# Turning the second experts' rows among the last output tiles, moving the gathered sums, and storing in four parts

## The chip, the cores and the metric

The kernel runs on one core of one Trainium2 chip. The metric is the device time in microseconds. Before the change it is 1516.37 us, the median of three runs (1516.31 to 1519.39).

## What is computed

The input is 1250 nodes with 512 features, and 40,000 edges sorted by their target. Four blocks follow each other, each added to its own input:

```python
x = x + _L0_gnn_ref(_layernorm(x), edge_index_t)      # means over segments, copied back
x = x + _L0_ffn_ref(_layernorm(x)[None], ...)[0]      # 8 experts of width 1536, top 2
x = x + _L1_gnn_ref(_layernorm(x), edge_attr_4, edge_attr_8, edge_index, ...)
x = x + _L1_ffn_ref(_layernorm(x)[None], expert_weights, expert_indices, w1, w2)[0]
```

The change lies in the last two. The third block forms eight blocks of 128 message features per edge, sums them by target node, and multiplies the sums by two output matrices:

```python
msg0 = segment_sum(m0, receiver); msg1 = segment_sum(m1, receiver)
o0, o1 = _lin_irreps(msg0, msg1, W_out0, W_out1)
out = concatenate([o0, o1.reshape(num_nodes, 3 * MUL)], -1) / 10
```

The fourth block has only 512 drawn assignments of two experts each, so only the first 512 nodes get something from it:

```python
for e in range(8):
    h = gelu(xg @ w1[e])                              # 512 -> 256
    y = where(bin_ids == e, h @ w2[e], y)             # 256 -> 512
out = zeros((T, hs)).at[token_ids].add(w * y)
```

## The kernel before

The five engines have one instruction list each (`vector`, `scalar`, `tensor`, `gpsimd`, `sync`), written out by hand, and each runs its list in order. Semaphores set the order between engines; there is no planner. Nodes lie in ten tiles of 128 rows (`NT` = 10), the last with 98. `T5` = 4 is the number of tiles that the second experts work on.

**The edge loop** (lines 1029 to 1041, 1719 to 1736 and others) goes through 88 steps. Each step forms messages for 512 edges from node rows that GpSimd gathers into four buffers of 128 x 1024 values, `gat_pair` (line 328), and sums them with products on TensorE. VectorE adds each step's sum to a running one, and SyncE writes each running sum to the DRAM tensor `sums` (line 2111).

**The output tiles.** When the loop is through, GpSimd gathers for each node tile the rows of `sums` that belong to it, in three buffers `sums_in` in turn (line 1956). TensorE transposes a gathered tile in eight blocks (`turn_sums`, line 1772), ScalarE copies the result out of PSUM in two halves (line 1426), and TensorE forms 16 products with the output weights (`out_products`, line 1780) and a last product in two parts that brings in one extra row (line 1801). VectorE adds the result to `xs`, in two operations of different layout (lines 1089 and 1093). TensorE's list has `turn_sums` of tile t + 1 ahead of the products of tile t, so it doesn't wait for ScalarE's copy of the tile at hand. Banks 0 to 3 of PSUM hold turned sums, banks 4 and 5 the outputs.

After tile 3, the last of the four that the second experts need, VectorE runs the layer norm of these four (`layer_norm(range(T5))`, lines 441 to 480), ScalarE takes the square root for it, and both split the first expert's weights in a high and a low part (lines 1405, 1411, 1065, 1073). Products of 32-bit floats are formed in three passes over such parts (`PASSES`).

**Turning the second experts' rows.** Behind the last output tile, TensorE transposes the four normed tiles `ln[:, t]`, four blocks each (line 1810), into banks 0 and 1 in turn. ScalarE copies each to the high half of `x_hl` (called `nodes_hl` in the profile, line 1435), and VectorE subtracts that from the bank to get the low half (line 1106). From the third tile on TensorE waits for the subtraction of the tile but one before, whose bank it takes.

**The second experts.** TensorE then waits until all four low halves are there and all ten tiles' outputs are added (`v_xt`, `v_o`). For each of eight experts it forms two hidden halves of 12 products each (line 1822), which ScalarE puts through a gelu and copies (lines 1443, 1447) and VectorE subtracts from (line 1125); then 24 products for the four output tiles (line 1833), in banks 4 to 7 in turn, which VectorE multiplies by the coefficient and adds to `xs` (line 1134). The coefficients are made by 17 small operations (lines 1111 to 1118) behind the last subtraction. SyncE stores rows 512 and up when all ten outputs are added (lines 2117, 2119), and the first 512 rows in one transfer when all additions of all experts are done (line 2127); then it waits for all stores.

`phase_tensors` gives out SBUF of a phase: tensors of different calls lie over each other, from the same address. `sums_in` and the two `edge_weights` tensors came from one such call, `x_hl` and its neighbours from another, so gathered sums and turned rows shared memory. `spin` (line 1453) issues products whose result nobody reads.

Of the kernel before, what the change touches and what calls it, by code (L numbers as in the profile page):

```python
# [8 lines left out]
F32 = mybir.dt.float32  # L9
# [3 lines left out]
ALU = mybir.AluOpType  # L13
ACT = mybir.ActivationFunctionType
# [3 lines left out]
NP, NT = 128, 10  # L18
# [25 lines left out]
NTILE = -(-((NE - NW) // TILE + NW) // BT) * BT  # L44
STEPS = NTILE // Q
# [5 lines left out]
MUL, HID = 128, 64  # L51
SILU_2MOM = 1.679177
T1, E1, H1 = 512, 8, 256
T5 = T1 // NP
# [7 lines left out]
NGAT, NSUM, NPICK, NHOT, HOT_STEPS = 8, 3, 3, 2, 4  # L62
# [3 lines left out]
NORMS = (range(0, 3), range(3, 6), range(6, NT))  # L66
LATE_ROWS = 4
MLP_AT = 4
PASSES = ((0, 0), (0, 1), (1, 0))
CHUNKS = [("up", b, k) for b in range(HB) for k in range(4)] + [("down", b, k) for b in range(HB) for k in (0, 2)]  # L70
NCH = len(CHUNKS)
# [7 lines left out]
def search_tree():  # L79

    lo, hi, levels = np.array([0]), np.array([NE]), []
    for _ in range(SEARCH_LEVELS):
# [10 lines left out]
              ident=128, ones=128, before=128, valid=NT, part=1, quarter_tile=STEPS + 2, quarter_hot=Q, node_in=1,  # L93
# [59 lines left out]
def program(nc, consts, x, anc, sub, leaf_table, src, dst, ea4, ea8, gate, w13, w2, w_up, w_mlp1, w_mlp23,  # L153
            w_mlp4, w_out, ew, ei, v1, v2, out):
    ctx = ExitStack()
    with ctx:
# [28 lines left out]
        def phase_tensors(**sizes):  # L185

            with ExitStack() as phase:
                return [phase.enter_context(nc.sbuf_tensor(n, [128, words], dt))[:, :]
                        for n, (words, dt) in sizes.items()]

        pairs = [ctx.enter_context(nc.psum_tensor(f"pair{i}", [128, 1024], F32)) for i in range(4)]
        banks = [pair[:, h * 512:(h + 1) * 512] for pair in pairs for h in range(2)]
# [3 lines left out]
        for name, w in CONSTS.items():  # L196
            K[name] = cst[:, at:at + w]
            at += w
        ident, ones, before = K["ident"], K["ones"], K["before"]
        xs_at = top[0]  # L200
        xs = carve(NT * D).rearrange("p (t d) -> p t d", t=NT)
        ln_at = top[0]
        pair_row = carve(NT * ROW).rearrange("p (t d) -> p t d", t=NT)
        ln, node_id, first_pick = pair_row[:, :, 0:D], pair_row[:, :, D].bitcast(I32), pair_row[:, :, D + 1]
# [32 lines left out]
                for i in range(4)]  # L237
# [31 lines left out]
                                           for _ in range(5))  # L269
# [24 lines left out]
        _, other_up1b, other_down0 = phase_tensors(other_gap0=(4096, F32), other_up1b=(2048, F32),  # L294
                                                   other_down0=(2048, F32))
        _, other_down1 = phase_tensors(other_gap1=(2048, F32), other_down1=(2048, F32))
# [7 lines left out]
        late = zone_of(lnT_at + 4 * NPAD - LATE, LATE)  # L304
        wup_sb, m23_sb, m4_sb, wo_sb = late(2 * MUL), late(2 * HID), late(512), late(512)

        *sums_in, w_copy0, w_copy1 = phase_tensors(**{f"sums_in{i}": (8 * MUL, F32) for i in range(3)},
                                                   edge_weights0=(2 * MUL, F32), edge_weights1=(2 * MUL, F32))
        w_copy = (w_copy0, w_copy1)
        recs = carve(NREC * REC, edge_at).rearrange("p (s c) -> p s c", c=REC)  # L310
        table = dram("node_table", [N, 4 * MUL])
# [6 lines left out]
        ring = zone_of(zone, ZONE - 2048)  # L318
# [6 lines left out]
        msg_pair = [m.rearrange("p (t b u) -> p t b u", t=2, b=8) for m in msg_pair]  # L325
        run_sum = [ring(8 * MUL) for _ in range(NSUM)]
        act1, act2, fT, act3 = ring(512), ring(512), ring(128), [ring(512) for _ in range(2)]
        gat_pair = [ring(1024).rearrange("p (t m u) -> p t m u", t=2, m=4) for _ in range(NGAT // 2)]
        sums = dram("sums", [STEPS * NP, 8 * MUL])
        sum_pair, tp_pair, mlp_pair = pairs[0], pairs[1:3], pairs[3]  # L330
        tp_bank = banks[2:6]
# [6 lines left out]
        x_hl, a1_hl, a2_hl, h_hl0, h_hl1 = phase_tensors(  # L338
            nodes_hl=(2 * 4 * T1, F32R), w_in_hl=(2048, F32R), w_out_hl=(2048, F32R), second_hidden_hl0=(1024, F32R),
            second_hidden_hl1=(1024, F32R))  # L340
        x_hl = x_hl.rearrange("p (s k n) -> p s k n", s=2, k=4)
# [23 lines left out]
        d_store = sem("stored")  # L365
# [69 lines left out]
        def vector(v):  # L435
# [225 lines left out]
            for lv in range(SEARCH_LEVELS - TOP):  # L661
                n = 2 ** lv
# [406 lines left out]
            def split_out(e):  # L1069
                v.wait_ge(a_w2, e + 1)  # L1070
                if e:
                    v.wait_ge(p_y, T5 * e)
                v.tensor_tensor(out=a2_hl[:, 1].rearrange("p k d -> p (k d)"), in0=e_w[e % 2][:, 1024:2048],
                                in1=a2_hl[:, 0].rearrange("p k d -> p (k d)").bitcast(F32),
                                op=ALU.subtract).then_inc(v_w2, 1)
# [6 lines left out]
            v.tensor_copy(out=extra_out, in_=banks[4][:, :]).then_inc(v_extra, 1)  # L1082
            T.wait()
            out_scale = (SILU_2MOM / 8) / 16 / 10
            for t in range(NT):
                r, bank = rows(t), banks[4 + (t + 1) % 2]
                v.wait_ge(p_o, t + 1)
                T.wait()
                T.did(v.scalar_tensor_tensor(out=xs[:r, t, 0:MUL], in0=bank[:r, 0:MUL], scalar=out_scale,
                                             in1=xs[:r, t, 0:MUL], op0=ALU.mult, op1=ALU.add))  # L1090
                xv = xs[:r, t, MUL:].rearrange("p (u m) -> p m u", m=3)
                T.wait()
                T.did(v.scalar_tensor_tensor(out=xv, in0=bank[:r, MUL:].rearrange("p (m u) -> p m u", m=3),  # L1093
                                             scalar=out_scale, in1=xv, op0=ALU.mult, op1=ALU.add), v_o, t + 1)
                if t < T5:
                    block_stats(t)
                if t == T5 - 1:
                    layer_norm(range(T5))
                    split_in(0)
                    split_out(0)  # L1100


            for t in range(T5):
                v.wait_ge(a_xt, t + 1)
                T.wait()
                T.did(v.tensor_tensor(out=x_hl[:, 1, :, t * NP:(t + 1) * NP],  # L1106
                                      in0=banks[t % 2][:, :].rearrange("p (k n) -> p k n", k=4),
                                      in1=x_hl[:, 0, :, t * NP:(t + 1) * NP].bitcast(F32), op=ALU.subtract), v_xt, t + 1)
            v.wait_ge(d_ew, 32)
            T.wait()  # L1110
            T.did(v.tensor_copy(out=ei_sb, in_=ei_sb.bitcast(I32)))
# [27 lines left out]
        def scalar(a):  # L1139
# [279 lines left out]
            for u in range(NT + 1):  # L1419
                a.wait_ge(p_sums_T, u + 1)  # L1420
                if u == 2:
                    a.wait_ge(p_extra, 1)
                if u > 2:
                    a.wait_ge(p_o, u - 2)
                for h in range(2):
                    done = a.activation(out=sums_T[u % 2][:, h * 512:(h + 1) * 512], in_=banks[2 * (u % 2) + h][:, :],  # L1426
                                        func=ACT.Copy)
                done.then_inc(a_sums_T, 1)
                if u == T5 + 1:
                    root(range(T5))  # L1430
                    split_in(0)
                    split_out(0)
            for t in range(T5):
                a.wait_ge(p_xt, t + 1)
                a.activation(out=x_hl[:, 0, :, t * NP:(t + 1) * NP],
                             in_=banks[t % 2][:, :].rearrange("p (k n) -> p k n", k=4),
                             func=ACT.Copy).then_inc(a_xt, 1)
            for e in range(E1):
                for h in range(2):
                    a.wait_ge(p_h, 2 * e + h + 1)  # L1440
# [11 lines left out]
        def tensor(pe):  # L1452
# [312 lines left out]
            def turn_sums(u):  # L1765
                if u:
                    pe.wait_ge(d_sin[(u - 1) % 3], 16 * ((u - 1) // 3 + 1))
                rows_in = sums_in[(u - 1) % 3] if u else run_sum[(STEPS - 1) % NSUM]
                if u >= 2:
                    pe.wait_ge(a_sums_T, u - 1)  # L1770
                for b in range(8):
                    tr = pe.transpose(out=banks[2 * (u % 2) + b // 4][:, b % 4 * 128:(b % 4 + 1) * 128],  # L1772
                                      in_=rows_in[:, b * 128:(b + 1) * 128], identity=ident)
                tr.then_inc(p_sums_T, 1)

            def out_products(bank, u, last=True):
# [5 lines left out]
                                       start=k == n == 0, stop=True, skip_group_check=True)  # L1782
                return mm

            turn_sums(0)
            pe.wait_ge(a_sums_T, 1)
            out_products(banks[4], 0).then_inc(p_extra, 1)
# [2 lines left out]
            for t in range(NT):  # L1790
                bank = banks[4 + (t + 1) % 2]
                if t + 2 <= NT:
                    turn_sums(t + 2)
                pe.wait_ge(a_sums_T, t + 2)
                if t >= 2:
                    pe.wait_ge(v_o, t - 1)
                out_products(bank, t + 1)
                if t == 0:
                    pe.wait_ge(v_extra, 1)
                    pe.wait_ge(v_ehot, 1)  # L1800
                pe.matmul(out=bank[:, :], lhsT=extra_hot[:, t * NP:(t + 1) * NP], rhs=extra_out, start=False,  # L1801
                          stop=True, skip_group_check=True).then_inc(p_o, 1)


            for t in range(T5):
                pe.wait_ge(v_norm, NT // 2 + t + 1)
                if t >= 2:
                    pe.wait_ge(v_xt, t - 1)
                for k in range(4):
                    tr = pe.transpose(out=banks[t % 2][:, k * 128:(k + 1) * 128], in_=ln[:, t, k * 128:(k + 1) * 128],  # L1810
                                      identity=ident)
                tr.then_inc(p_xt, 1)
            pe.wait_ge(v_xt, T5)
            pe.wait_ge(v_o, NT)
            for e in range(E1):
# [22 lines left out]
        def gpsimd(g):  # L1838
# [108 lines left out]


            g.wait_ge(v_sumrow, 1)
            g.wait_ge(d_zero, 32)  # L1950
            for q in range(NSUM):
                g.wait_ge(d_sum[q], 16 * ((STEPS - 1 - q + NSUM - 1) // NSUM))
# [7 lines left out]
        def sync(s):  # L1960
# [161 lines left out]
            for e in range(2, E1):  # L2122
                s.wait_ge(v_w1, e - 1)
                s.wait_ge(v_w2, e - 1)
                load_second(e)
            s.wait_ge(v_y, E1 * T5)
            s.dma_start(out=out[0:T5 * NP].rearrange("(t p) d -> p t d", p=NP), in_=xs[:, 0:T5]).then_inc(d_store, 16)
            s.wait_ge(d_store, 48)
            s.wait_ge(d_fill, 16)
            s.wait_ge(d_zero, 32)  # L2130

# [55 lines left out]
```

## Time and profile before

| | before |
|---|---|
| median of 3 runs | 1516.37 us |
| the profiled execution | 1517.24 us |
| its span | 1515.4 us |
| mean granted clock of TensorE | 0.966 |
| TensorE busy | 1378.3 us (91%) |
| VectorE busy | 1207.7 us (80%) |
| ScalarE busy | 1026.6 us (68%) |
| GpSimd busy | 990.2 us (65%) |
| data moved by DMA | 316.66 MB |

The profile is of one execution, which took 1517.24 us; the span of 1515.4 us lies between its first and its last recorded instruction. The chain of waits goes back from the last instruction, at each step to what released it. PE is TensorE, PEld its weight loads, DVE VectorE, ACT ScalarE, POOL GpSimd, SP SyncE. The granted clock is a share of full speed, 1.00 being 2.4 GHz and 0.50 being 1.2 GHz.

### The profile page before, as it was taken

The page shows a single profiled execution, that of the slowest core. Times are in us where ns is not written, and L with a number is a line of the kernel's source. Part 1 is how long each engine was busy: PE and PEld are TensorE (multiplying, and loading weights), DVE is VectorE, ACT ScalarE, POOL GpSimd, SP SyncE. Part 2 cuts the span into 40 slices and gives each one's busy share as a digit, 9 for nine tenths or more (in the row PEclk, how much of TensorE's full clock was granted, in tenths as well). Part 3 has the DMA queues.
Part 4 walks back from the last instruction along what each step waited for, and adds up shares of the span by engine and source line. Part 5 has one row for each costly group of instructions (what it writes and reads, how often), then busy time and mean ns, then how long its engine had stood idle before and what let it go on. Part 6 is the DMA issues. An engine that isn't in the chain of part 4 may idle for free. (4 is left out here: it accounts for less than half of the span.)

```text
span 1515.4 us, 26210 instructions
## 1 busy us (share of the span) xinstructions
PE 1378.3 (91%) x8774; PEld 837.2 (55%) x8774; DVE 1207.7 (80%) x1633; ACT 1026.6 (68%) x2442; POOL 990.2 (65%) x850
## 2 busy tenths in 40 slices
PE   5858989998899989999896899999999999988998
PEld 3545737885388846887384533333333333336786
DVE  7888818995299936998198499999999999995464
ACT  6347718884288825887183689989989888883343
POOL 4136647888688888888871278878887888772000
PEclk9859999999899999999999999999999999999999
DMA  9338393559445955473523588888888888885321
GB/s 338 133 154 269 106 372 87 162 175 381 125 134 166 346 191 176 138 261 110 184 52 122 174 263 274 285 277 277 277 283 265 277 272 279 277 269 171 115 86 56
DMA packets 90990, 316.66 MB, mean 209 GB/s; under 512 B 23642, under 2 KB 25876, under 8 KB 80747
## 3 DMA queue, kind: packets, MB, share of 16 engines
q1 hardware_dynamic: 45208, 202.57, 36.1%
q0 software_dynamic: 45648, 112.41, 27.8%
q8 instruction: 71, 1.16, 0.3%
q14 instruction: 63, 0.52, 0.1%
HBM read 378.96 MB, written 77.16 MB: 301 GB/s over the span
## 5 line engine op out<-in xcount | busy, mean ns | idle before, releaser
L1883 POOL DMA_INDIRECT sorted_edges<-arena x320 | 473.3, 1479 | 105.5 <-issue 97.7
L898 DVE TENSOR_TENSOR weights_hl<-arena,weights_hl 128x1024 fp32r<-128x1024 f32 x342 | 405.2, 1222 | 62.4 <-ACT weights_hl L1222 59.7
L1930 POOL DMA_INDIRECT arena<-node_table,arena x352 | 337.5, 959 | 135.2 <-issue 40.5
L1222 ACT ACTIVATE weights_hl<-arena 128x1024 fp32r<-128x1024 f32 x342 | 351.9, 1059 | 46.7 <-PE pair L1582 46.5
L1380 ACT ACTIVATE arena<-arena 128x32 f32<-128x32 bf16 x1408 | 359.0, 342 | 2.1 <-DVE arena L1008 2.1
L1582 PE MATMUL pair<-weights_hl,rows_hl 128*128 128x512 f32 x1368 | 326.2, 396 | 4.4 <-DVE rows_hl L903 1.7
L1029 DVE TENSOR_TENSOR arena<-pair,arena 128x768 f32<-128x768 f32 x352 | 317.9, 942 | 0.0
L1582 PEld LDWEIGHTS pair<-weights_hl,rows_hl 128*128 128x128 f32 x1368 | 251.8, 188 | 70.1 <-DVE weights_hl L898 10.6
L1719 PE MATMUL pair<-arena 64*128 64x512 f32 x704 | 189.8, 627 | 24.2 <-DVE arena L1029 23.4
L1582 PE MATMUL pair<-weights_hl,hidden_hl 128*128 128x512 f32 x684 | 165.8, 396 | 0.0
L917 DVE TENSOR_TENSOR arena<-pair,arena 128x512 f32<-128x512 f32 x69 | 47.3, 685 | 125.3 <-ACT arena L1260 97.5
L1582 PEld LDWEIGHTS pair<-weights_hl,hidden_hl 128*128 128x128 f32 x684 | 125.0, 188 | 25.5
L1736 PE MATMUL pair<-arena 128*32 128x256 f32 x2112 | 131.3, 379 | 0.0
L1260 ACT ACTIVATE arena<-pair 128x512 f32<-128x512 f32 x69 | 41.4, 599 | 125.1 <-PE pair L1619 111.3
L1736 PEld LDWEIGHTS pair<-arena 128*32 128x32 f32 x2112 | 75.4, 110 | 77.1 <-issue 51.5
L1719 PEld LDWEIGHTS pair<-arena 64*128 64x128 f32 x704 | 56.8, 187 | 106.1 <-ACT arena L1316 42.2
L1041 DVE SCALAR_TENSOR_TENSOR arena<-arena,pair 128x1024 f32<-128x1024 f32 x88 | 111.3, 1265 | 3.4 <-PE pair L1736 3.4
L1619 PE MATMUL pair<-arena 128*64 128x512 f32 x352 | 96.6, 661 | 18.2 <-DMA arena<-in_w 18.2
L1733 PE MATMUL pair<-arena 128*32 128x512 f32 x704 | 94.6, 608 | 14.4 <-POOL arena L1919 6.9
L1022 DVE TENSOR_TENSOR arena<-pair,arena 128x512 f32<-128x512 f32 (+1 forms) x176 | 95.6, 543 | 12.8 <-DMA arena<-node_table,arena 10.7
L1893 POOL DMA_INDIRECT node_sums<-arena x27 | 55.1, 2040 | 58.9 <-ACT arena L1268 51.9
L1919 POOL TENSOR_TENSOR arena<-edge_weights,arena 128x256 f32<-128x256 f32 x88 | 66.7, 758 | 5.9 <-DMA arena<-node_table,arena 4.4
(289 smaller groups left out, 1531.4 us busy)
## 6 DMA issues: line engine op xcount, KB each, us to landing
arena<-in_w SPq DMA_DIRECT2D x77, 2048.0 KB, 11.5
arena<-in_w SPq DMA_DIRECT2D x77, 1024.0 KB, 8.3
sums<-arena SPq DMA_DIRECT2D x88, 512.0 KB, 6.9
other_down<-in_w SPq DMA_DIRECT2D x8, 1024.0 KB, 10.4
arena<-in_v SPq DMA_DIRECT2D x16, 512.0 KB, 4.6
pair_rows<-arena SPq DMA_DIRECT2D x1, 5934.0 KB, 26.3
arena<-pair_rows SPq DMA_DIRECT2D x23, 256.0 KB, 3.5
arena<-node_table,arena POOLq DMA_INDIRECT x352, 4.8
```

Of the source, the lines that this page charges most:

```text
L898: v.tensor_tensor(out=part[s][:, 1], in0=by_chunk(n)[4], in1=part[s][:, 0].bitcast(F32), op=ALU.subtract).then_inc(v_low, 1)
L1022: v.tensor_tensor(out=m[:, 0:n, 0:2], in0=tp[:, :].rearrange("p (t w u) -> p t w u", t=2, w=4)[:, 0:n, 0:2], in1=rows_in[:, 0:n, 0:1].to_b ...
L1029: v.tensor_tensor(out=m[:, t, 2:8].rearrange("p (w m) u -> p w m u", w=2), in0=w34.unsqueeze(2).to_broadcast([128, 2, 3, MUL]), in1=rows_i ...
L1041: v.scalar_tensor_tensor(out=run_sum[s % NSUM], in0=run_sum[(s - 1) % NSUM], scalar=g_same[:, s:s + 1], in1=sum_pair[:, :], op0=ALU.mult, ...
L1222: a.activation(out=part[s][:, 0], in_=cols, func=ACT.Copy).then_inc(a_high, 1)
L1380: done = a.activation(out=picks[s % NPICK][:, j, c], in_=hot[s // HOT_STEPS % NHOT][:, :, s % HOT_STEPS, j], func=ACT.Copy, scale=recs[:, ...
L1582: mm = pe.matmul(out=bank[:, :], lhsT=st[:, a], rhs=part[s][:, w, half * 512:(half + 1) * 512], start=begins and (a, w) == (0, 0), stop=en ...
L1619: mm = pe.matmul(out=banks[2 + 2 * s + c][HALF * h:HALF * (h + 1), :], lhsT=xS[:, at:at + HALF], rhs=w[:, c], start=k == 0, stop=k == 3, s ...
L1719: pe.matmul(out=tp_bank[(i + h) % Q], lhsT=act3[batch % 2][p, k * 128:(k + 1) * 128], rhs=m4_sb[p], start=True, stop=True).then_inc(p_tp, 1)
L1736: mm = pe.matmul(out=bank.rearrange("p (b u) -> p b u", b=4)[:, c - 1:4:4 - c], lhsT=pick, rhs=m[:, 0:c + 5:c + 4], start=c == 1, stop=Tru ...
L1883: g.indirect_dma_start(out=sorted_edges, out_offset=bass.IndirectOffsetOnAxis(ap=slot_i[:, j:j + 1], axis=0), in_=er[:, j, :], in_offset=N ...
L1930: g.indirect_dma_start(out=row, out_offset=None, in_=table, in_offset=bass.IndirectOffsetOnAxis(ap=senders[:, i:i + 1], axis=0)).then_inc( ...
```

## The change

The four turns move into the loop over output tiles, one behind each of the tiles 5 to 8 (`TURNS_AT`), on all three engines; they use banks 6 and 7. The three `sums_in` buffers become the first three of the four buffers of gathered node rows, since the turned rows are now written while sums are still being gathered, and GpSimd waits for the last messages before it gathers. The final store is four transfers of 128 rows, each behind its own additions.

```diff
+TURNS_AT = (5, 6, 7, 8)
...
-        *sums_in, w_copy0, w_copy1 = phase_tensors(**{f"sums_in{i}": (8 * MUL, F32) for i in range(3)},
-                                                   edge_weights0=(2 * MUL, F32), edge_weights1=(2 * MUL, F32))
+        w_copy0, w_copy1 = phase_tensors(edge_weights0=(2 * MUL, F32), edge_weights1=(2 * MUL, F32))
...
-        gat_pair = [ring(1024).rearrange("p (t m u) -> p t m u", t=2, m=4) for _ in range(NGAT // 2)]
+        gat_rows = [ring(8 * MUL) for _ in range(NGAT // 2)]
+        gat_pair = [g.rearrange("p (t m u) -> p t m u", t=2, m=4) for g in gat_rows]
+        sums_in = gat_rows[0:3]
... VectorE
+            def low_second(t):
+
+                v.wait_ge(a_xt, t + 1)
+                T.wait()
+                T.did(v.tensor_tensor(out=x_hl[:, 1, :, t * NP:(t + 1) * NP],
+                                      in0=banks[6 + t % 2][:, :].rearrange("p (k n) -> p k n", k=4),
+                                      in1=x_hl[:, 0, :, t * NP:(t + 1) * NP].bitcast(F32), op=ALU.subtract), v_xt, t + 1)
+
             for t in range(NT):
...
                     layer_norm(range(T5))
                     split_in(0)
                     split_out(0)
-
-
-            for t in range(T5):
-                v.wait_ge(a_xt, t + 1)
...
+                if t in TURNS_AT:
+                    low_second(TURNS_AT.index(t))
... ScalarE, in the loop over u, behind the copies of turned sums
                 done.then_inc(a_sums_T, 1)
+                if u - 2 in TURNS_AT:
+                    t = TURNS_AT.index(u - 2)
+                    a.wait_ge(p_xt, t + 1)
+                    a.wait_ge(g_msg, STEPS)
+                    a.activation(out=x_hl[:, 0, :, t * NP:(t + 1) * NP],
+                                 in_=banks[6 + t % 2][:, :].rearrange("p (k n) -> p k n", k=4),
+                                 func=ACT.Copy).then_inc(a_xt, 1)
... TensorE
+            def turn_second(t):
+
+                pe.wait_ge(v_norm, NT // 2 + t + 1)
+                if t >= 2:
+                    pe.wait_ge(v_xt, t - 1)
+                for k in range(4):
+                    tr = pe.transpose(out=banks[6 + t % 2][:, k * 128:(k + 1) * 128], in_=ln[:, t, k * 128:(k + 1) * 128],
+                                      identity=ident)
+                tr.then_inc(p_xt, 1)
...
                           stop=True, skip_group_check=True).then_inc(p_o, 1)
-
-
-            for t in range(T5):
-                pe.wait_ge(v_norm, NT // 2 + t + 1)
...
+                if t in TURNS_AT:
+                    turn_second(TURNS_AT.index(t))
... GpSimd, ahead of the gathers of the sums
             g.wait_ge(v_sumrow, 1)
+            g.wait_ge(v_msg, NTILE)
... SyncE
-            s.wait_ge(v_y, E1 * T5)
-            s.dma_start(out=out[0:T5 * NP].rearrange("(t p) d -> p t d", p=NP), in_=xs[:, 0:T5]).then_inc(d_store, 16)
-            s.wait_ge(d_store, 48)
+            for t in range(T5):
+                s.wait_ge(v_y, E1 * T5 - T5 + t + 1)
+                s.dma_start(out=out[t * NP:(t + 1) * NP], in_=xs[:, t]).then_inc(d_store, 16)
+            s.wait_ge(d_store, 16 * (2 + T5))
```

## Rows read from the trace of the kernel before

**Rows 1.** Chain of waits, 1410 us to the end: start, duration, engine and line.

```profile
1415.63 0.30 DVE arena L1089
1415.96 0.69 DVE arena L1093
...
1419.66 0.70 DVE nodes_hl L1106
...
1420.41 7.35 PE pair L1822 x24
1427.76 5.44 PE pair L1833 x24
...
1503.92 5.45 PE pair L1833 x24
...
1509.40 0.75 DVE arena L1134
```

**Rows 2.** Timeline of TensorE, 1412 to 1430 us; idle time before and releaser bracketed.

```profile
1415.43 1.04 PE L1810 MATMUL pair<-arena 128*128 128x128 f32 x8
1417.58 0.63 PE L1810 MATMUL pair<-arena 128*128 128x128 f32 x4 [1.11 <-DVE nodes_hl L1106]
...
1420.41 7.35 PE L1822 MATMUL pair<-nodes_hl,w_in_hl 128*128 128x512 f32 x24 [1.41 <-DVE nodes_hl L1106]
```

**Rows 3.** Chain of waits, 1400 to 1412 us: output tiles 6 and 7.

```profile
1403.03 2.02 PE pair L1780 x16
...
1405.91 0.87 PE pair L1772 x8
1406.78 1.79 PE pair L1780 x16
...
1409.43 0.87 PE pair L1772 x8
```

**Rows 4.** Timeline of VectorE, 1366 to 1432 us.

```profile
1402.20 0.68 DVE L1093 SCALAR_TENSOR_TENSOR arena<-pair,arena 128x384 f32<-128x384 f32 x1
```

**Rows 5.** Groups of VectorE's instructions, 1420 to 1425 us: busy time, mean ns, idle.

```profile
L1114 DVE SCALAR_TENSOR_TENSOR arena<-arena 128x8 f32<-128x8 f32 x8 | 1.3, 167 | 0.3
```

**Rows 6.** Timeline of ScalarE, 1366 to 1432 us.

```profile
1410.34 1.08 ACT L1426 ACTIVATE arena<-pair 128x512 f32<-128x512 f32 x2 [2.44 <-PE pair L1772]
...
1419.04 0.60 ACT L1435 ACTIVATE nodes_hl<-pair 128x512 fp32r<-128x512 f32 x1 [0.20 <-PE pair L1810]
```

**Rows 7.** Stretches: length, busy us (instructions) per engine, granted clock, DMA share, GB/s.

```profile
1416.30:1420.40 4.10, 1.43 (x10) 0.84 (x8) 3.10 (x5) 2.80 (x5) 0.00 (x0) 1.00 0.69 260
1370.70:1374.60 3.90, 1.16 (x12) 0.91 (x9) 2.08 (x2) 1.08 (x2) 2.35 (x3) 1.00 0.18 24
1420.40:1424.00 3.60, 3.59 (x9) 2.83 (x10) 2.80 (x17) 0.53 (x1) 0.00 (x0) 0.53 1.00 284
```

**Rows 8.** Timeline of SyncE's DMA issues, 1340 us to the end.

```profile
1435.63 0.33 SPq L2033 DMA_DIRECT2D arena<-in_v  x1
1436.01 0.43 SPq L2034 DMA_DIRECT2D arena<-in_v  x1
...
1510.18 0.39 SPq L2127 DMA_DIRECT2D out<-arena  x1
```

**Rows 9.** Stretches of the final store, columns as in rows 7.

```profile
1511.10:1514.10 3.00, 0.00 (x0) 0.00 (x0) 0.00 (x0) 0.00 (x0) 0.00 (x0) 0.77 0.92 350
1512.00:1512.50 0.50, 0.00 (x0) 0.00 (x0) 0.00 (x0) 0.00 (x0) 0.00 (x0) 1.00 1.01 385
```

**Rows 10.** DMA issues of the whole span: count, KB each, median us to landing.

```profile
arena<-in_v SPq DMA_DIRECT2D x16, 512.0 KB, 4.6
node_table<-arena SPq DMA_DIRECT2D x9, 256.0 KB, 2.1
```

**Rows 11.** Waits of SyncE, 1330 us to the end: us in total, times, longest.

```profile
SPq L156 <- DMA out<-arena: 4.4, 1, 4.4
```

**Rows 12.** Timeline of GpSimd, 1340 to 1432 us.

```profile
1371.65 1.36 POOL L1956 DMA_INDIRECT sums_in<-sums,arena  x1 [6.26 <-DMA sums<-arena]
```

More of the change, by code:

```diff
@@ L1100, in vector @@
                     split_out(0)
-            for t in range(T5):
-                v.wait_ge(a_xt, t + 1)
[L1105 to L1108, printed above, removed]
+                if t in TURNS_AT:
+                    low_second(TURNS_AT.index(t))
             v.wait_ge(d_ew, 32)
@@ L1432, in scalar @@
                     split_out(0)
-            for t in range(T5):
[L1434 to L1437, printed above, removed]
             for e in range(E1):
@@ L1802, in tensor @@
                           stop=True, skip_group_check=True).then_inc(p_o, 1)
-            for t in range(T5):
-                pe.wait_ge(v_norm, NT // 2 + t + 1)
[L1807 to L1812, printed above, removed]
+                if t in TURNS_AT:
+                    turn_second(TURNS_AT.index(t))
             pe.wait_ge(v_xt, T5)
```

## The prediction

> **What bounds the kernel now.** I read the chain of waits first, then the timelines of the engines in its last stretch, then stretches with the granted clock, and the transfers last. The change touches only what follows the edge loop, from about 1371 us on, so what counts is what releases each step there.
>
> In the chain [rows 1], the last output tile ends on TensorE at 1415.6 and VectorE's two additions for it run to 1416.65. Then the layer-normed rows of the second experts are turned in strict steps (TensorE transposes, ScalarE copies the high part, VectorE subtracts for the low part). The last subtraction ends at 1420.36 and TensorE starts the first expert's product at 1420.41. From there the chain is TensorE alone: groups of 24 products, the first taking 7.35 us and the next fifteen 5.44 us each (the first and last of the fifteen are shown). At 1509.40 the last addition begins; it ends at 1510.15, and what remains is the store.
>
> **Turning among the tiles (lines 1810, 1435, 1106).** After the last additions TensorE waits 1420.41 - 1416.65 = 3.76 us for turned rows. The change puts the four turns behind tiles 5, 6, 7 and 8.
>
> - TensorE. Two turns, eight transposes, took 1.04 us in the timeline [rows 2]; followed directly by other work, eight transposes of the same shape take 0.87 in the chain [rows 3]. So a turn is 0.44 us, and four put 4 x 0.44 = 1.76 us ahead of the last tile's end. Tile 6 gives some back: its 16 products took 2.02 us instead of 1.79 [rows 3], since they waited for VectorE's additions of tile 4, which ended at 1402.20 + 0.68 = 1402.88 [rows 4]. The first turn now stands ahead of them and covers these 0.23. The last tile moves by 1.76 - 0.23 = 1.53 us.
> - The result. VectorE's last additions start at 1415.63 + 1.53 = 1417.16, last 1.02 as before and end at 1418.18; TensorE, which waits for them before the first expert, starts at 1418.23, 2.2 us earlier. Lower bound: each turn costs what one that stands alone does, 0.63 us [rows 2], and tile 6 gives nothing back; then the last tile moves 2.52 us and 1.2 are gained. Upper bound: the turns join as the two did, saving the 0.17 by which 1.04 exceeds 0.87: 2.4.
> - Cover on ScalarE. It now waits for a turn ahead of its next copies of turned sums. A tile with a turn is 3.52 + 0.44 = 3.96 us [rows 3]; in it ScalarE has its two copies, 1.08, and the new one, 0.60 [rows 6]. TensorE needs the copies one tile later, so the wait holds up nothing.
> - Cover on VectorE. Its subtraction waits for ScalarE's copy, behind the same tile's additions: 1.02 + 0.70 [rows 1] = 1.72 of 3.96 us. Queued behind it are the next tile's additions. The tightest is the last: tile 8 ended at 1409.43 + 3.52 = 1412.95 and now ends at 1412.95 + 1.53 - 0.44 = 1414.04; turn, copy and subtraction then run to 1415.8, before 1417.16. It costs nothing while it ends by then; every microsecond past that is on the path.
> - VectorE's coefficient operations, 17 of some 0.17 us [rows 5], follow its last additions as before, some 3.4 us with hand-overs. They end at 1421.6, and the first gelu's copy isn't ready before 1418.23 + 2.72 + 1.2 = 1422.1.
>
> **The clock.** From 1416.3 to 1420.4 TensorE is busy 1.43 of 4.1 us, and in 1420.4 to 1424.0 the granted clock is 0.53 [rows 7]: of the two levels, 2.4 and 1.2 GHz, the lower one. That is the first group's 7.35 against 5.44. After the change TensorE has one pause there, from 1417.2 to 1418.2, with unbroken work on both sides. Rows for a pause like it: from 1370.7 to 1374.6 TensorE was busy only 1.16 of 3.9 us and the clock was 1.00 throughout [rows 7]. So I take the first group as 5.44 plus 0.16 for the start after a pause, as 1.04 stood to 0.87: a gain of 1.75. Bounds: 0, if the clock falls all the same, and 1.91. The hidden units behind it stay covered: gelu, copy and subtraction, 0.6 + 0.6 + 0.7 by rows of the same shape [rows 1, 6], against 2.72 us of products for the other half.
>
> **Four stores in place of one (line 2127).** Now: issue at 1510.18 [rows 8], data moving in 1511.1 to 1514.1 [rows 9], SyncE released 4.4 us after its issue of 0.39 [rows 11], so at 1515.0, and the end at 1515.4. 1024 KB at the middle rows' 385 GB/s are 2.72 us, a quarter 0.68. In the new form the first three leave as their additions end; these come as fast as three products of 5.44 / 24, that is every 0.68 us, so each store's data are through when the next one's start, and an issue of 0.39 fits between. The fourth has the issue time that the one has now. Two sizes for its landing: today's less three quarters of the data, 4.8 - 2.04 = 2.76 us; or the nine writes of the very same shape, 2.1 us from issue to landing [rows 10]. Gains: 2.04 and 2.7. As three others have just kept the queue busy, I take 2.2, near the first. The bound on the other side, starts and receipts paid in sequence, is a rival below.
>
> The Trainium skill ("DMA: Bandwidth & Descriptors", Anatomy of one DMA) gives each transfer a fixed cost of about 2.0 us beside its bytes at 436 GB/s: an estimate by it is 4.4 us for the one store and 2.6 for a quarter, a gain of 1.8. It speaks against the split if the fixed cost is paid four times in a row; the trace doesn't bear that out, as its loads issued in pairs 0.38 us apart land in the usual time [rows 8, 10].
>
> **The gathered sums' new place, and new waits.** The sums are gathered where the edge loop's rows lay, so GpSimd waits for the last messages. It waited already for the write of the sums of the last step but one [rows 12], which SyncE issues after VectorE closed that step, and VectorE's own order puts that behind all messages. So the new wait is met whenever the old one is: 0. Behind it are only the gathers. ScalarE's new wait, for GpSimd's last product, is met by the last step's sum, for which it waited already: 0. Reading another address: the same number of partitions and bytes; I take 0, with a bound of 0.17 either way per tile that I can't exclude, the difference that two turns showed [rows 2, 3], so 1.7 over ten tiles.
>
> **Sum.** Against the profiled execution (1517.24 us, span 1515.4): 2.2 + 1.75 + 2.2 = 6.15, so 1511.1, span 1509.3. The median shown is 0.87 below this execution's time: 1516.37 - 6.15 = **1510.2**. A measurement of this kernel can tell about 0.2%, 3.0 us, from no change: the marks are 1513.3 and 1519.4.
>
> **Rivals.**
> - The clock still falls. For: in 1416.3 to 1420.4 it was lost with no single pause over 1.41 us [rows 2, 7]. Against: the emptier stretch from 1370.7 kept it. 1510.2 + 1.75 = 1512.0. Chance 0.12.
> - The four stores go one after another, each with its own start and receipt. The first leaves at 1508.1 by today's times; 4 x 2.1 to 4 x 2.76 end at 1516.5 to 1519.1 instead of 1515.0: 1.5 to 4.1 lost where I count 2.2 gained, so 1513.9 to 1516.5, the middle 1515.2, within 0.2%. Against: the pairs of loads. Chance 0.06. The page's fixed cost, paid four times with the bytes, makes 10.4 us by estimate.
> - It doesn't do what it says: a wait in the tile loop, or a slower read of the sums, gives back what the turns free and the clock with it. For: the in-order queues of ScalarE and VectorE. Against: the slack above. Only the stores are left, 1516.4 - 2.2 = 1514.2. Chance 0.04.
> - Slower: the tile loop becomes serial. Place: lines 1772 to 1801, where TensorE would wait for turn, copy, subtraction and additions in each of four tiles, 0.44 + 0.61 + 0.70 + 1.02 = 2.77 us, 11.1 in all. Removed are 3.76; the stores give 2.2, the clock nothing. Net +5.1: 1521.5. It passes the upper mark from 2.25 us open per turn. Against: TensorE asks for a subtraction only two turns later. Chance 0.03.
>
> **How the numbers follow.** Forecast 0.75, rivals 0.12, 0.06, 0.04, 0.03. Faster by over 0.2%: 0.75 + 0.12 = 0.87; within 0.10; slower 0.03. Range: the upper bounds together, 2.4 + 1.91 + 2.7 = 7.0, give 1509.4, and 0.3 for the spread of a median makes 1509.1; the other way it takes in the lost clock, 1512.0, and the lower bound of the turns, 1.0 more: 1513.0.
>
> **What would show it.** Right: line 1810's transposes stand between lines 1801 and 1772 without a new pause over 0.1 us; the first group of line 1822 starts near 1418.2 and the next group 5.6 later, the granted clock 1.00 from 1418 to 1424; four issues come some 0.7 apart, and the span ends 3.0 to 3.2 us after the last addition instead of 5.25. Wrong: the last tile ends after 1417.6 (turns dearer), a clock near 0.5 in the first group, an end more than 3.6 us after the last addition, or a start that has moved before 1371.

## The result, and the profile after

The changed kernel took 1512.01 us, the median of eight runs (1510.42 to 1517.61); the kernel before, run beside it, 1518.51 us (1516.22 to 1521.02). The ratio is 0.9966, with a 95% interval of 0.9953 to 0.9979: 5.2 us less, between 3.2 and 7.1. (The ratio is not that of the two medians, which lie 6.5 us apart.) A second set of twelve runs gave 0.9964 (0.9950 to 0.9977). The forecast, 0.41% less, lies in both intervals; the profiled executions differ by 6.0 us in span, where it said 6.15. The time of 1512.01 is 1.8 us above the forecast of 1510.2, inside the range of 1509.1 to 1513.0.

The chain of waits of the changed kernel, at the places of [rows 1] and [rows 3]; L1789 is the old L1780, L1820 the old L1801, L1800 the old L1810, L1835 and L1846 the experts' products:

```profile
1402.16 0.44 PE pair L1800 x4
1402.60 0.87 PE pair L1781 x8
1403.47 1.79 PE pair L1789 x16
1405.26 0.86 PE pair L1820 x2
...
1414.04 0.44 PE pair L1800 x4
1414.48 1.79 PE pair L1789 x16
1416.26 0.86 PE pair L1820 x2
1417.12 1.13 issue
1418.25 5.70 PE pair L1835 x24
1423.96 5.44 PE pair L1846 x24
...
1500.12 5.45 PE pair L1846 x24
...
1505.59 0.75 DVE arena L1141
```

Each turn costs 0.44 us of TensorE. Tile 6's products take 1.79, no longer 2.02. The first expert starts at 1418.25 instead of 1420.41, its first group takes 5.70 us instead of 7.35, and the last addition ends at 1506.34 instead of 1510.15. What stands between 1417.12 and 1418.25 is the wait for the last tile's additions.

The granted clock (the column before the DMA share), for [rows 7]:

```profile
1416.50:1418.00 1.50, 0.62 (x2) 0.00 (x0) 0.81 (x2) 0.00 (x0) 0.00 (x0) 1.00 0.00 0
1418.00:1424.00 6.00, 5.75 (x25) 4.80 (x26) 3.64 (x19) 1.24 (x3) 0.00 (x0) 1.00 0.82 252
```

The timelines of ScalarE and VectorE around the last turn, for [rows 6] and [rows 4]:

```profile
1411.43 1.08 ACT L1433 ACTIVATE arena<-pair 128x512 f32<-128x512 f32 x2 [0.28 <-PE pair L1781]
1414.51 0.60 ACT L1440 ACTIVATE nodes_hl<-pair 128x512 fp32r<-128x512 f32 x1 [2.00 <-PE pair L1800]
```
```profile
1415.20 0.69 DVE L1092 TENSOR_TENSOR nodes_hl<-pair,nodes_hl 128x512 fp32r<-128x512 f32 x1
1417.16 0.29 DVE L1100 SCALAR_TENSOR_TENSOR arena<-pair,arena 98x128 f32<-98x128 f32 x1 [1.27 <-PE pair L1820]
```

ScalarE waits 2.00 us for the last turn and VectorE is through 1.27 us before the next tile's products come: the slack the forecast counted on. (The additions on L1100 that start at 1417.16 are those of the last tile.) The store, for [rows 8, 11]: SyncE's issues, then its waits.

```profile
1504.33 2.37 SPq L2142 DMA_DIRECT2D out<-arena  x4
```
```profile
SPq L157 <- DMA out<-arena: 2.2, 1, 2.2
```

The four issues span 2.37 us, the last is through at 1506.70, and 2.2 us later, half of the 4.4 before, the data have landed. The span ends 3.06 us after the last addition instead of 5.25.

So the 6.0 us of the two profiles are 2.16 (start of the first expert), 1.65 (its first group) and 2.19 (the store).

### The profile page after: what moved, and what is told of

Same layout as the page of the kernel before. It is cut to its first block, busy times and chain, and to the rows that moved or that the text cites. A ratio compares the mean times of both kernels' runs of the same rounds, so it can differ in the third digit from the quotient of the medians.

```text
span 1509.4 us, 26218 instructions
## 1 busy us (share of the span) xinstructions
PE 1376.8 (91%) x8774; PEld 837.9 (56%) x8774; DVE 1208.3 (80%) x1633; ACT 1026.0 (68%) x2442; POOL 989.1 (66%) x850
## 4 chain that ended last, share of the span: by engine, by line
PE 54%; DVE 18%; DMA 15%; POOL 7%; issue 5%; ACT 1%; DVEq 0%; SPq 0%; POOLq 0%; ACTq 0%
PE pair L1591 31%; DMA arena<-node_table,arena 11%; DVE arena L1031 7%; POOL arena L1943 5%; PE pair L1628 4%; DMA arena<-in_w 4%; PE pair L1835 3%; PE pair L1846 3%; PE pair L1643 3%; PE pair L1582 2%; POOL arena L1932 2%; PE pair L1745 1%; PE pair L1789 1%; PE pair L1728 1%; DVE arena L1024 1%
```

## The experiments

The kernels of one batch ran on one chip beside the kernel before: the first four, the next four, the last four. Medians and ratios are of 7 to 12 runs of the kernel in question; `e11` and `e12` are single executions. Each profile is of one execution.

**Turns without the stores.** `e1` is the changed kernel with the old end:

```diff
-            for t in range(T5):
-                s.wait_ge(v_y, E1 * T5 - T5 + t + 1)
-                s.dma_start(out=out[t * NP:(t + 1) * NP], in_=xs[:, t]).then_inc(d_store, 16)
+            s.wait_ge(v_y, E1 * T5)
+            s.dma_start(out=out[0:T5 * NP].rearrange("(t p) d -> p t d", p=NP), in_=xs[:, 0:T5]).then_inc(d_store, 16)
```

> The changed kernel with the single final store put back (1024 KB behind all additions). Theory 1, the parts add: the first expert's product starts near 1418.2 on this trace's clock (2.2 us earlier than before), its first group takes 5.7 us, and the span ends 5.2 to 5.3 us after the last addition as before, so 3.8 us less than before and 2.2 us more than the changed kernel. Theory 2, the tail's gain is mostly the store: less than 2 us below before. Theory 3, the stages ahead of 1371 us make the runs of one kernel differ by as much as 5 us: the spread over rounds is then as wide as the whole gain, whatever the tail does.

Measured: 1515.24 us against 1517.84, ratio 0.9980 (0.9970 to 0.9990), 3.0 us less (1.5 to 4.6); 3.8 were expected. The end comes 5.32 us after the last addition and the first group takes 5.69 us, both as theory 1 has them. But the first expert starts 47.61 us after the edge loop's last sum instead of 46.13. The chain shows where:

```profile
1376.12 1.09 ACT arena L1433 x2
1377.26 3.54 PE pair L1789 x16
1380.79 1.72 PE pair L1465 x4
```
```profile
1376.00:1380.00 4.00, 2.75 (x13) 2.75 (x14) 0.00 (x0) 1.08 (x2) 0.94 (x1) 0.62 0.92 336
```

The first 16 output products took 3.54 us where the profiles before and after have 2.05: in this execution the clock fell here, 1.5 us, behind the pauses around the first turned sums. The code there is the same in all kernels. And the loop's last sum itself ended at 1374.79, 2.7 us later than in those profiles. Without these 1.5 us the tail, from the loop's last sum to the end, would be 139.5 us against 143.3 before: the 3.8 us of theory 1. The interval of the times by itself doesn't exclude theory 2. Theory 3 holds too: the eleven runs spread over 4.9 us.

**Stores without the turns.** `e2` is the kernel before with the other half of that diff.

> The kernel before with only the final store in four transfers. Theory 1: the end comes 3.0 to 3.1 us after the last addition instead of 5.25, so 2.2 us less than before; the chain up to the last addition is that of before, the first expert's group 7.35 us long. Rival, starts and receipts paid in sequence: the end 6.7 to 9.3 us after the last addition, 1.5 to 4.1 us more than before.

Measured: 1517.01 us, ratio 0.9988 (0.9977 to 0.9998), 1.8 us less (0.3 to 3.5). The end comes 3.09 us after the last addition; SyncE waits 2.2 us after its four issues. A line of its chain and one of SyncE's waits:

```profile
1422.74 8.58 PE pair L1822 x24
```
```profile
SPq L156 <- DMA out<-arena: 2.2, 1, 2.2
```

The rival, payment in sequence, falls. The first group took 8.58 us in this execution, for the same turns as before; the granted clock was 0.50 from 1422 to 1428.

**Only the pauses filled.** `e3` is the kernel before with one filling product each behind the second and the fourth turn:

```diff
                 tr.then_inc(p_xt, 1)
+                if t % 2:
+                    spin(1, banks[6])
             pe.wait_ge(v_xt, T5)
```

> The kernel before with one filling product (result unread, bank 6) behind the second and the fourth turn, in TensorE's pauses of 1.1 and 1.4 us; nothing else moves. Theory A, the clock fell because TensorE was idle during the turns: the granted clock stays 1.00 from 1416 to 1428, the first expert's first group takes 5.4 to 5.7 us instead of 7.35, and the kernel is 1.65 to 1.9 us faster than before. Theory B, the clock would fall there in any case, by the load that begins at 1420: the group stays at 7.3 and the time at that of before, or up to 0.5 us above.

In the timeline of TensorE the fillings are L1456:

```profile
1415.35 1.04 PE L1810 MATMUL pair<-arena 128*128 128x128 f32 x8
1416.22 1.02 PE L1456 MATMUL pair<-arena 128*128 128x512 f32 x2
1417.51 0.63 PE L1810 MATMUL pair<-arena 128*128 128x128 f32 x4 [0.27 <-DVE nodes_hl L1106]
1418.31 0.63 PE L1810 MATMUL pair<-arena 128*128 128x128 f32 x4 [0.17 <-DVE nodes_hl L1106]
1418.77 1.02 PE L1456 MATMUL pair<-arena 128*128 128x512 f32 x2
1420.35 5.76 PE L1824 MATMUL pair<-nodes_hl,w_in_hl 128*128 128x512 f32 x24 [0.55 <-DVE nodes_hl L1106]
```
```profile
1420.00:1424.00 4.00, 3.65 (x16) 3.02 (x17) 3.09 (x18) 1.45 (x2) 0.00 (x0) 1.00 1.00 301
```

The first group takes 5.76 us at full clock, while the DMA share is 1.00 as it was before, so the load on the DMA isn't what lowers the clock. In the profile, loop's end to the last addition is 136.5 us against 138.1. This profile is as theory A has it. The timed runs don't settle it: 1516.46 us, ratio 0.9996 (0.9987 to 1.0005), at most 2.0 us less and at most 0.8 more, with 1.65 to 1.9 less expected by theory A and 0 to 0.5 more by theory B. And one execution is thin evidence, since `e5` below has a first group of 5.78 us with its pauses unfilled.

**The last wait moved.** `e4` is the changed kernel with this, which takes away the pause of 1.13 us:

```diff
             pe.wait_ge(v_xt, T5)
-            pe.wait_ge(v_o, NT)
             for e in range(E1):
...
                     mm.then_inc(p_h, 1)
+                if e == 0:
+                    pe.wait_ge(v_o, NT)
                 pe.wait_ge(v_w2, e + 1)
```

> The changed kernel with TensorE's wait for all ten tiles' additions moved behind the first expert's hidden products, which use banks 2 and 3 and not the outputs' banks. Theory 1: the pause of 1.13 us ahead of the first expert goes, its first group starts as tile 9's products end near 1417.1 and takes 5.44 us, 0.2 less than after a pause: 1.1 to 1.4 us less than the changed kernel. Rival: VectorE's coefficient operations now stand in front of the first hidden subtraction, which comes 0.4 us later than it could; if TensorE waits for it, the gain is 0.7 to 1.0.

The chain of this kernel; L1834 and L1847 are the experts' two groups:

```profile
1419.27 0.86 PE pair L1820 x2
1420.13 5.46 PE pair L1834 x24
1425.59 5.61 PE pair L1847 x24
```

No pause is left and the first group takes 5.46 us, but the second takes 5.61 instead of 5.44: VectorE's coefficient operations hold up the first hidden subtraction, as the rival had it, by 0.17 us only (it ends at 1425.35, and TensorE's weight loads for the second group start at 1425.47, after 0.30 us idle). The time: seven runs, 1513.04 us, ratio 0.9969 (0.9958 to 0.9980). The changed kernel's ratio in the first pair is 0.9966, so the 1.1 to 1.4 us don't show in the times, though nothing in the intervals excludes them. In this profile too the first output products were slow, 3.42 us.

**Only the place.** `e5` is the kernel before with the gathered sums in the loop's buffers and GpSimd's new wait, the diff's lines for these and no others.

> The kernel before with only the gathered sums moved to the edge loop's buffers and GpSimd's new wait. Theory 1: nothing changes. Gathers are issued at the same distance from the loop's end and from each other (3.52 us), the output tiles take 3.52 us each, and the time is within 0.05% of before. Rival, a slower place: turned sums or gathers take longer, up to 0.17 us per tile, 1.7 us in all.

Measured: 1520.83 us against 1519.08, ratio 1.0008 (0.9993 to 1.0022). The timeline of GpSimd:

```profile
1391.70 0.94 POOL L1958 DMA_INDIRECT arena<-sums,arena  x1 [2.58 <-PE pair L1773]
1395.22 0.94 POOL L1958 DMA_INDIRECT arena<-sums,arena  x1 [2.58 <-PE pair L1773]
```

The gathers are 3.52 us apart, as before. The profile speaks for theory 1. The times don't bear out its 0.05%: the ratio is 0.08% above 1, and the interval reaches from 1.1 us less to 3.3 us more, so the rival's 1.7 us stay open. This execution was of another kind than the first profile: the clock fell at the first output products (3.27 us), and not at the first expert, although the turns stand there as before:

```profile
1424.18 5.78 PE pair L1823 x24
```

This leaves a rival that no run here tests. All five profiles with bare turns and the old place of the sums have a slow first group; `e5`, the only one with bare turns and the new place, has not. The changed kernel has the new place too, so its 1.65 us might come in part from there. `e3` speaks against it, a fast first group at the old place, but by one execution.

**The turns one tile later.** `e6` has `TURNS_AT = (6, 7, 8, 9)` and ScalarE's last copy behind its loop.

> The changed kernel with the four turns behind tiles 6, 7, 8 and 9 instead of 5 to 8; the last copy stands behind ScalarE's loop. One turn is open again: turn, copy and subtraction stand behind tile 9's products and additions. Theory 1: tile 9's products end 0.44 us earlier, at 44.56 us after the loop's end instead of 45.0; VectorE adds until 45.6, subtracts until 46.4, and TensorE's first expert starts 0.3 us later than in the changed kernel, after a pause of 1.0 us between the turn and the first expert. Clock 1.00 throughout, the first group 5.7. Rival, the clock: with a turn and a pause there it falls again, the group takes over 7 us.

Measured: 1514.43 us in ten runs, ratio 0.9970 (0.9953 to 0.9986). The first expert starts 46.72 us after the loop's end, 0.59 later than in the changed kernel:

```profile
1408.61 2.02 PE pair L1793 x16
...
1422.86 0.68 DVE arena L1104
1423.57 0.02 DVEq L130
1423.63 0.70 DVE nodes_hl L1092
1424.38 5.74 PE pair L1839 x24
```

Of the 0.59, 0.3 are the open subtraction, as expected, and 0.23 tile 6's products, again at 2.02 because no turn stands in front of them. I had left that out here, though the forecast had counted it. Clock and group stay: with a turn and a pause of about 1.4 us in that place it did not fall. The first of the four turns is best put where it covers a wait; by the times alone, 0.9970 and 0.9964 to 0.9966, the two places can't be told apart.

**The pauses at the loop's end filled as well.** `e7` is `e4` with this:

```diff
                         weights_of(i)
+                        if i == NTILE - Q:
+                            spin(2, banks[6])
...
+            spin(1, banks[6])
             pe.wait_ge(a_p4, 1)
...
             turn_sums(0)
+            spin(1, banks[6])
             pe.wait_ge(a_sums_T, 1)
```

> The changed kernel with the wait for the additions moved behind the first hidden products, and with filling products in three pauses that TensorE has at the loop's end: two within the last step (pause 2.0 us), one ahead of the first turned sums (1.5 us), one behind them (1.25 us). Theory C, the clock falls at these pauses in some executions and not in others, and this makes up part of what is missing against the forecast: the granted clock is 1.00 from 1350 us to the last product, the first output products take 2.05 us and not 3.4 to 3.5, and the mean over the runs is 1 to 2 us lower than that of the changed kernel with only the late wait, so 0.45 to 0.5% below before. Theory D, the fillings only delay what they stand in front of: the same or up to 1 us slower than the late wait alone, although the clock stays up.

Measured: 1512.71 us against 1519.08 in seven runs, ratio 0.9947 (0.9927 to 0.9966). The same batch's mean of twelve runs of the changed kernel is 1514.7, that of these seven 1512.0. It is the fastest of all kernels here in its ratio and in its tail, 136.1 us from the loop's end to the end. Its first output products took 2.05 us. Its tail is 1.2 us shorter than the 137.3 of the changed kernel without a fall: that is what the late wait is worth, within the 1.1 to 1.4 expected of `e4`. In the profiles theory D falls, since `e7`'s tail is 1.6 us shorter than `e4`'s. The times lean to C without settling it: the intervals of `e4` and `e7` overlap, and they ran in different batches.

**The changed kernel again.**

> The changed kernel once more, for more executions of both kernels on one chip. If the tail's gain of 6.0 us in the first pair of profiles is what the change brings, and the rest is chance, the ratio is 0.9960 with an interval of 0.001 to either side. If the change gives something back elsewhere, it stays at 0.9966 or above.

Measured: 1515.06 us against 1519.08, twelve runs, ratio 0.9964 (0.9950 to 0.9977); here the medians are only 4.0 us apart. Both outcomes lie in that interval, so the question of something given back stays open. In its profile the first output products took 3.40 us, and the span from the loop's end to the end was 138.7 us where the first profile had 137.3: the 1.35 us are that fall.

**Both kernels with the filled start.** `e9` and `e10` are the kernels before and after with the three fillings of `e7`.

> The kernel before with the filling products at the loop's end and around the first turned sums (two, one and one), nothing else. Theory E, the clock's two falls in this tail are alternatives: an execution that loses it near 1376 us keeps it at the first expert, and the other way round. Without the first place it falls at the first expert in nearly every execution: the first group takes 7.3 to 8.6 us in the profile, the output products 2.05, and the mean time is that of the kernel before or up to 1 us less. Theory F, the two falls have nothing to do with each other: the mean is 1 to 1.7 us below the kernel before.

> The changed kernel with the same fillings. By theory E the changed kernel's only open place for the clock in the tail was the one now filled; the first group takes 5.7 us, from the loop's end to the end are 137.3 us, and it is 6.0 us or more (0.40%) under the filled kernel before, which is what the forecast worked out, where the unfilled pair differs by 5.2 to 5.5. By theory F both filled kernels gain alike and differ by what the unfilled pair does.

This batch ran on a chip on which the kernel before takes 1628.8 us. Ratios: `e9` 0.9999 (0.9976 to 1.0023), `e10` 0.9959 (0.9941 to 0.9978). From the loop's end to the end: 143.4 and 137.3 us, 6.1 apart, with first groups of 7.35 and 5.69 us. The size is the forecast's, but the intervals are too wide to tell theory E from F. The next two profiles, both of the kernel before, are for that.

> One more profile of the kernel before, to see where the clock falls in its tail. By theory E: either near 1376 us and then a first group of 5.7 us, or not there and then a first group of 7.3 to 8.6; from the loop's end to the end 143.3 to 144.6 us.

> The same once more, with the same two outcomes by theory E; both falls in one execution, or none, would speak against it.

`e11`: first output products 2.05 us, first group 7.26, 143.3 us from loop's end to end. `e12`, in two pieces of its chain:

```profile
1486.35 3.68 PE pair L1780 x16
```
```profile
1533.86 7.36 PE pair L1822 x24
```

Both falls in one execution, and 145.0 us. Theory E, that they are alternatives, falls.

Where the tail's clock fell, by profile (us; the tail is from VectorE's last running sum to the end of the span):

| kernel | first 16 output products | first group | last addition to end | tail |
|---|---|---|---|---|
| before | 2.05 | 7.35 | 5.25 | 143.3 |
| before, `e11` | 2.05 | 7.26 | 5.27 | 143.3 |
| before, `e12` | 3.68 | 7.36 | 5.30 | 145.0 |
| `e5`, place only | 3.27 | 5.78 | 5.35 | 143.5 |
| `e2`, stores only | 2.05 | 8.58 | 3.09 | 142.4 |
| `e9`, before, filled start | 2.05 | 7.35 | 5.34 | 143.4 |
| `e3`, before, filled pauses | 2.05 | 5.76 | 5.31 | 141.8 |
| changed | 2.05 | 5.70 | 3.06 | 137.3 |
| changed, `e8` | 3.40 | 5.72 | 3.12 | 138.7 |
| `e1`, turns only | 3.54 | 5.69 | 5.32 | 141.0 |
| `e6`, turns later | 2.05 | 5.74 | 3.10 | 137.9 |
| `e10`, changed, filled start | 2.05 | 5.69 | 3.09 | 137.3 |
| `e4`, late wait | 3.42 | 5.46 | 3.05 | 137.7 |
| `e7`, late wait, filled | 2.05 | 5.45 | 3.10 | 136.1 |

## Why the prediction was right, and where it was not

- **The turns.** Right: 0.44 us a turn, tile 6's 0.23 given back, the last additions start at 1417.16 (forecast 1417.16), the first expert at 1418.25 (1418.23).
- **The cover on ScalarE and VectorE.** Right: ScalarE's wait for the turn, VectorE's for the copy and TensorE's for the subtraction are in place, and none is on the path: in the chain each turn is followed by the next work without a pause, down to 1417.12.
- **The clock.** Right in size for the first pair of profiles, 1.65 for 1.75, and probably in cause (`e3`, and seven fast first groups of seven with moved turns); the new place of the sums as part of the cause isn't excluded. But I took the loss from one execution as a constant. With bare turns, six profiles have first groups of 7.35, 8.58, 5.78, 7.35, 7.26 and 7.36, mean 7.28: a gain of 1.6 on average and between 0.1 and 2.9 in one execution. The first rival, a fall that stays after the change, didn't come in any of seven profiles with moved turns; that its 1512.0 is the measured 1512.01 is chance. The row held against it, the stretch from 1370.7 that kept the clock, was luck: in five of eleven profiles the clock fell right behind that same stretch.
- **The stores.** Right: 2.19 for 2.2; overlap, not sequence. From the start of its issue the last quarter took 0.4 + 2.2 = 2.6 us: nearer the 2.76 of the forecast's first size than the 2.1 of the writes of 256 KB [rows 10], which count from the same point. The estimate from the Trainium skill ("DMA: Bandwidth & Descriptors", Anatomy of one DMA), whose fit was measured on transfers that GpSimd issues, was a gain of 1.8; for these transfers of SyncE the trace shows 2.19.
- **The new place and waits.** The gathers and tiles of `e5`'s profile show no cost. Its times leave the forecast's bound of 1.7 us open on the slow side.
- **The step that failed is the term for the spread, "0.3 for the spread of a median".** It was too small, and it stood only at the fast end of the range, 1509.1; at the slow end, 1513.0, the spread was put at nothing. 1516.37 was a median of three. With eight runs, these three among them, the median beside the changed kernel was 1518.51, 2.1 us higher; the later batches gave 1517.84 and 1519.08, and 1628.8 on the slow chip. So the forecast of 1510.2 takes a difference that the intervals bear out from a base that was 1.5 to 2.7 us low. The measured 1512.01 lies in the range, but the measured ratio on the measured base, 0.9966 of 1518.51, is 1513.3 and lies just outside it. The term should have been about 2 us, at both ends. What makes the spread is in part shown: the last sum of the loop ends between 1372.0 and 1377.7 us in nine profiles of the same instructions up to there, and in five of the eleven profiles without fillings at the loop's end the first output products took 3.3 to 3.7 us instead of 2.05, which put off the first expert by 1.3 to 1.7 us. What moves the loop's end I did not look into.
- **The missing microsecond.** 5.2 and 5.5 us by the ratios, 6.0 by the first profiles. The profiled tails of the three before-like and the three changed-like kernels with an open start average 143.9 (before, `e11`, `e12`) and 138.3 (changed, `e8`, and `e1` less 2.2), 5.6 apart. That is argued from a few executions; the intervals hold the forecast and don't ask for a cause.

## What to carry to other kernels

A strict chain of small steps over three engines, at the seam between two phases, can be moved into the loop ahead of it, one step of the chain per pass, if each engine has more slack in a pass than its step takes; look for a tile that waits anyway and put the first step in front of it. The seam cost twice here, 3.76 us by its wait, of which the move won back 2.2, and 1.65 by the clock that TensorE lost in it, and in the one profile that tried it a filling product in each pause returned the second part. A store that ends a kernel is worth cutting so that just the last piece comes after the last result: 2.2 us here. And a single profile prices a clock loss for one execution: for a change of 0.4%, first see how far two profiles of the same kernel differ.

## What the runs showed of the hardware

The clock can fall, or not, at the same pauses of the same code: around the first turned sums in five of eleven executions, at the first expert in five of six. A single pause of 1.1 us (changed kernel) or 1.4 us (`e6`) did not lower it in any of the five profiles that have it. What TensorE did in these places differs by more than the pause: in the kernel before it ran nothing but transposes between the last tile's products and the first expert, for 4.80 us, and likewise for 3.8 us between the loop's last products and the first output products; in the changed kernel it had 1.13 us between products, in `e6` 1.87 with one turn in them. Which of this decides isn't tested.

One chip, that of the last batch, was 7% slower. Between the first and the last of the 88 running sums, 875.8 to 1370.8 us in the first profile and 886.1 to 1482.8 in `e11`, lie 102 of the 112 us. There VectorE's running sum (L1041), which must wait for the DRAM write of the sum three steps ago, waited 76.3 us in all, against none in the first profile; the tail took the same time as elsewhere. The idle time ahead of this line in `e11`, and in the kernel before's first profile:

```profile
L1041 DVE SCALAR_TENSOR_TENSOR arena<-arena,pair x88: 1268/1280/1281, 886.1 to 1482.8; 128x1024 f32<-128x1024 f32 x88
...
  remote: 76.3, 38
  PE pair L1736: 12.8, 25
```
```profile
L1041 DVE SCALAR_TENSOR_TENSOR arena<-arena,pair x88: 1260/1264/1281, 875.8 to 1370.8; 128x1024 f32<-128x1024 f32 x88
...
  PE pair L1736: 3.4, 2
```

That "remote" is this write's landing is read from the code, not tested.
